# The last attention stage of a two-layer block: block 0's queries placed by TensorE, and the router and wide products of the end spread over the last slots

## What is computed

```python
x = x + _L0_xattn_ref(_layernorm(x), ...)
x = x + _L0_ffn_ref(_layernorm(x), ...)
x = x + _L1_xattn_ref(_layernorm(x), ctx_2048, Wq, Wk, Wv)
x = x + _L1_ffn_ref(_layernorm(x), W, bias, rw1, rb1, rw2, rb2, A, B, gates)
# _L1_xattn_ref: 32 heads of 8 channels
q = _rmsnorm(q); k = _rmsnorm(k)
attn = softmax(einsum('bhnd,bhmd->bhnm', q, k) * 8 ** -0.5)
out = einsum('bhnm,bhmd->bhnd', attn, v)
# _L1_ffn_ref: the router, and the low-rank correction
h = silu(x @ rw1.T + rb1)
logits = (h @ rw2.T + rb2)[:, :16] + gates
topv, topi = top_k(logits, 2); sm = softmax(topv)
coeff = zeros_like(logits).at[rows, topi].set(sm)
base = x @ W.T + bias
xa = einsum('ni,eri->ner', x, A)
out = base + einsum('ner,eor->no', xa * coeff[:, :, None], B)
```

## Time and profile before

| | us |
|---|---|
| median of 3 runs (380.56 to 381.72) | 381.45 |
| the profiled execution's own time | 378.31 |
| its span, first to last instruction | 376.2 |
| busy in it: PE, DVE, ACT, POOL | 291.7, 274.7, 174.6, 100.8 |
| stage C, from its first query product to the last slot's last output product | about 251 to 337 |
| the end, to the span's end | about 337 to 376 |

### The profile page before, as it was taken

How to read it: one execution, slowest core, us unless ns; L and a number is a source line. 1 busy time by engine, 2 the same in 40 slices (tenths; PEclk the granted TensorE clock), 3 DMA queues, 4 the chain that set the end, 5 groups by cost and what they waited for, 6 DMA issues and landing times.

```text
span 376.2 us, 7252 instructions
## 1 busy us (share of the span) xinstructions
PE 291.7 (78%) x2636; PEld 182.2 (48%) x2636; DVE 274.7 (73%) x706; ACT 174.6 (46%) x296; POOL 100.8 (27%) x200
## 2 busy tenths in 40 slices
PE   4246888878887876899996998954888884978795
PEld 3112444344443333586775887831555552553543
DVE  6977789889898886778922643455588887686894
ACT  1102365665756666535333677413576665430101
POOL 1134254463543222202770211077101000000000
PEclk9855599999999999969996999985799999877999
DMA  7583359568585103100236477765756555100011
GB/s 248 159 260 113 92 159 281 155 194 274 151 255 154 46 24 134 46 2 21 92 112 195 133 254 263 262 186 161 218 161 198 172 157 164 49 3 0 0 56 56
DMA packets 70306, 53.20 MB, mean 141 GB/s; under 512 B 4864, under 2 KB 67072, under 8 KB 70272
## 3 DMA queue, kind: packets, MB, share of 16 engines
q1 hardware_dynamic: 64640, 41.76, 36.8%
q10 hardware_dynamic: 4096, 6.79, 5.7%
q0 software_dynamic: 1536, 4.20, 3.5%
HBM read 30.90 MB, written 21.63 MB: 140 GB/s over the span
## 4 chain that ended last, share of the span: by engine, by line
PE 38%; DVE 34%; DMA 8%; issue 8%; POOL 5%; ACT 4%; SPq 2%; DVEq 0%; POOLq 0%
DVE mx L1589 8%; PE psum L689 5%; PE psum L1027 4%; POOL sorted_x L1496 4%; PE psum L725 4%; PE psum L1040 4%; PE psum L674 3%; PE psum L710 2%; DVE pvT L1941 2%; DMA qstk<-mT 2%; ACT prob L1177 2%; PE psum L1003 2%; PE psum L816 2%; DVE rope_ab L1578 2%; PE psum L1136 2%
## 5 line engine op out<-in xcount | busy, mean ns | idle before, releaser
L1589 DVE TENSOR_REDUCE mx<-psum 128x2 f32<-128x512 f32 x128 | 81.3, 684 | 16.1 <-PE psum L689 15.3
L1177 ACT ACTIVATE prob<-psum 128x1024 f32<-128x1024 f32 x64 | 64.4, 1023 | 39.7 <-PE psum L710 39.4
L689 PE MATMUL psum<-kstk,qstk 64*128 64x256 bf16 x256 | 27.9, 300 | 26.7 <-DVE mx L1589 14.5
L725 PE MATMUL psum<-prob,vt 128*32 128x256 f32 x512 | 35.2, 392 | 6.2 <-ACT prob L1177 5.1
L1361 ACT ACTIVATE prob<-psum 128x1024 f32<-128x1024 f32 x32 | 31.9, 1019 | 13.2 <-PE psum L987 13.2
L689 PEld LDWEIGHTS psum<-kstk,qstk 64*128 64x128 bf16 x256 | 8.8, 98 | 43.6 <-DVE mx L1589 28.1
L484 POOL TENSOR_TENSOR parts<-qk_rest,parts 128x256 bf16<-128x256 f32 (+1 forms) x15 | 13.7, 913 | 51.0 <-ACT parts L1335 47.2
L710 PE MATMUL psum<-qstk,kstk 64*128 64x256 bf16 x256 | 25.1, 281 | 1.2 <-DMA qstk<-mT 1.2
L1003 PE MATMUL psum<-prob,vt 128*32 128x128 f32 x512 | 21.7, 292 | 4.6 <-ACT prob L1361 4.6
L725 PEld LDWEIGHTS psum<-prob,vt 128*32 128x32 f32 x512 | 14.2, 110 | 18.7 <-ACT prob L1177 7.6
L1027 PE MATMUL psum<-low,qstk 128*128 x124 | 18.6, 297 | 2.0 <-issue 1.9
(11 more groups left out here) (256 smaller groups left out, 610.2 us busy)
## 6 DMA issues: line engine op xcount, KB each, us to landing
qstk<-stack_scratch SPq DMA_DIRECT2D x32, 256.0 KB, 3.7
stack_scratch<-parts SPq DMA_DIRECT2D x23, 192.0 KB, 2.2
kstk<-key_scratch SPq DMA_DIRECT2D x16, 256.0 KB, 3.9
kstk<-stack_scratch SPq DMA_DIRECT2D x14, 256.0 KB, 5.7
stack_scratch<-parts SPq DMA_DIRECT2D x25, 128.0 KB, 2.1
low<-in_wup ACTq DMA_DIRECT2D x4, 640.0 KB, 4.6
wdn<-in_wdn ACTq DMA_DIRECT2D x4, 640.0 KB, 5.8
prob<-sorted_x SPq DMA_DIRECT2D x8, 256.0 KB, 4.3
```

The source lines that it names most:

```text
L689: last = nc.tensor.matmul(banks[s][:, nb * D:(nb + 1) * D], qstk[par][rows, pair, nb * P:(nb + 1) * P], kstk[par][rows, pair, :], start=Tr ...
L725: last = nc.tensor.matmul(pv_bank(1)[32 * j:32 * j + 32, g * D:(g + 1) * D], vt[b % 2][:, mb, 4 * t + j, 8:40] if low else vt[b % 2][:, mb ...
L1177: nc.scalar.activation(prob[(b * PAIRS + k) % 3][:], exp_buf(k).rearrange("p a n -> p (a n)"), ACT.Exp, scale=SCALE).then_inc(exp_done, 1)
L1589: nc.vector.tensor_reduce(mx[:, half, :, 4 * s + p4:4 * s + p4 + 1], bank.rearrange("n (b m) -> n b m", b=2), AX_X, ALU.max).then_inc(misc ...
```

## The change

Start of stage C:

- Block 0's queries no longer pass through DRAM. A table `place` of zeros and ones (GpSimd makes it early, beside `work_no`) is multiplied with each of the three parts by TensorE, 24 matmuls of 32 rows x 128 x 256 (`place_queries`), so that the stack's rows arise in PSUM, banks 4 to 7. ScalarE copies groups 0 and 2 and VectorE groups 1 and 3 into `qstk` (`stack_placed`). SyncE's loop over queries begins at block 1.
- The steps of `C_PRO` have PSUM banks of their own and another order: q of block 1 ahead of qT of block 0; qT of block 1 and xT of block 2 behind the placing; the first score product ahead of q of block 2. On VectorE the sums of squares stand ahead of `add_shared(2)`, and the statistics and centring of block 2 behind both copies of the stack.

Slots 5 to 7 and the end:

- The reciprocal root of the dense layer's norm starts from logarithm, exponential and square on ScalarE (`guess_ln`), with two steps on VectorE behind it (`ln_roots`) in place of ten. Statistics of blocks 0 to 3 are taken at slot 5's first spot, those of 4 to 6 in slot 7, block 7 alone behind the slots.
- Transposed blocks are copied by ScalarE (`take_dxT`) and not by VectorE. Wide products of blocks 0, 1 and 2 are made in slots 6 and 7, and ScalarE copies them out to SBUF (`take_wide`). The router's hidden layer is made for blocks 0 to 3, for 4 and 5, and for 6 and 7.
- GpSimd adds the bias and, for blocks 0 to 2, the base to `xall` (`based`). The two rows that were added to the logits one after the other are added to each other early.
- The order behind the slots is another on TensorE, ScalarE and VectorE.

```diff
-        C_PRO = [("v", 0), ("xT", 0), ("q", 0), ("xT", 1), ("qT", 0), ("q", 1), ("xT", 2), ("qT", 1), ("q", 2)]
+        C_PRO = [("v", 0), ("xT", 0), ("q", 0), ("xT", 1), ("q", 1), ("qT", 0), ("qT", 1), ("xT", 2), ("q", 2)]
+        C_GONE = [("v", 0), ("xT", 0), ("xT", 1), ("q", 0), ("qT", 0), ("q", 1), ("qT", 1), ("xT", 2), ("q", 2)]
+        C_BANK = {("v", 0): 4, ("xT", 0): 5, ("q", 0): 6, ("xT", 1): 0, ("q", 1): 1, ("qT", 0): 2, ("xT", 2): 3,
+                  ("qT", 1): 2, ("q", 2): 4 + (B_END + 8) % 2}
...
-        D_EARLY = {(5, 6): ("dxT", 0), (5, 7): ("dxT", 1), (6, 1): ("dxT", 2), (6, 2): ("dxT", 3),
-                   (6, 6): ("dh", 0), (7, 3): ("dlg", 0)}
+        D_EARLY = {(5, 5): ("dxT", 0), (5, 7): ("dxT", 1), (6, 1): ("dxT", 2), (6, 3): ("wide", 0), (6, 5): ("dxT", 3),
+                   (6, 7): ("dh", 0), (7, 1): ("wide", 1), (7, 3): ("dlg", 0), (7, 5): ("wide", 2)}
...
-            for b in range(NB):
+            for b in range(1, NB):
...
+            def place_queries(part, made):
+
+                pe.wait_ge(made, NB + 1)
+                for g, kp in itertools.product(range(4), range(2)):
+                    rows = slice(32 * g, 32 * g + 32)
+                    last = nc.tensor.matmul(psum[:, 4 + g, kp * D:(kp + 1) * D],
+                                            place[rows, part, 16 * kp:16 * kp + 16, :].rearrange("c l t -> c (l t)"),
+                                            parts[0][rows, 0, part, :], start=(part == 0 and kp == 0), stop=(part == 2),
+                                            skip_group_check=True)
+                    if part == 2 and kp == 1:
+                        last.then_inc(placed, 1)
...
+            pro_use("v", 0)
+            pro_use("xT", 0)
+            pro_use("q", 0)
+            pe.wait_ge(relu_done, 3 * N_SHARED)
+            pro_use("xT", 1)
+            pro_use("q", 1)
...
+            pro_use("qT", 0)
...
+            place_queries(0, hi_done)
+            place_queries(1, mid_done)
+            place_queries(2, lo_done)
+            pe.wait_ge(misc_free, pro_gone("q", 1))
+            pro_use("qT", 1)
+            pro_use("xT", 2)
...
             scores_c(0, 0)
+            pro_use("q", 2)
...
+            ring("dxT", 4)
+            ring("dxT", 5)
+            ring("dxT", 6)
+            ring("o")
...
-            pe.wait_ge(misc_free, C_END)
-            wide(0)
-            wide(1)
-            ring(("o",))
+            wide(3)
+            ring("dh", 1)
+            wide(4)
+            ring("dxT", 7)
+            ring("dh", 2)
+            wide(5)
+            ring("dlg", 1)
             pe.wait_ge(pv_free, 3 * NB + 2)
-            wide(2)
-            wide(3)
-            ring(("dxT", 4))
             flip_wxa(0)
-            ring(("dxT", 5))
             flip_wxa(1)
             delta(0)
-            ring(("dxT", 6))
+            delta(1)
+            wide(6)
             flip_wxa(2)
-            delta(1)
-            ring(("dxT", 7))
-            ring(("dh", 1))
             flip_wxa(3)
             delta(2)
+            ring("wide", 7)
             delta(3)
-            wide(4)
-            wide(5)
-            ring(("dlg", 1))
-            wide(6)
-            wide(7)
             flip_wxa(4)
...
+            squares(0, pro_full("q", 0), pro_bank("q", 0))
+            guess_roots(0)
+            squares(1, pro_full("q", 1), pro_bank("q", 1))
+            pro_split(0)
+            guess_roots(1)
+            for g in (0, 2):
+                stack_placed(g)
+            pro_split(1)
+            squares(2, pro_full("q", 2), pro_bank("q", 2))
+            guess_roots(2)
...
+            def take_wide(b):
+                key = slot_of("wide", b)
+                act.wait_ge(misc_full, late_full(key))
+                nc.scalar.copy(raw(b), late_bank(key)).then_inc(x_copied, 1)
...
+                nc.scalar.activation(ln_log[:, blocks], ln_v[:, blocks], ACT.Ln).then_inc(ln_step, 1)
+                act.wait_ge(ln_step, 3 * j + 1)
+                nc.scalar.activation(ln_g[:, 0, blocks], ln_log[:, blocks], ACT.Exp, bias=lead[:], scale=-0.5
+                                     ).then_inc(ln_step, 1)
+                act.wait_ge(ln_step, 3 * j + 2)
+                nc.scalar.activation(ln_g[:, 1, blocks], ln_g[:, 0, blocks], ACT.Square).then_inc(ln_step, 1)
...
+                    if shape == 5 and k == 3:
+                        guess_ln(0, 0, 4)
+                        take_dxT(0)
+                    if shape == 6 and k == 0:
+                        take_dxT(1)
+                    if shape == 6 and k == 1:
+                        take_dxT(2)
+                    if shape == 6 and k == 2:
+                        take_wide(0)
+                    if shape == 6 and k == 3:
+                        take_dxT(3)
...
+                        silu_exp(0)
+                    if shape == 7 and k == 1:
+                        take_wide(1)
                     if shape == 7 and k == 3:
+                        take_wide(2)
                         gap_exp(0)
...
+            guess_ln(1, 4, 3)
+            for b in range(4, 7):
+                take_dxT(b)
+            silu_exp(1)
+            guess_ln(2, 7, 1)
+            take_dxT(7)
+            silu_exp(2)
+            take_wxa(0)
+            take_wxa(1)
             gap_exp(1)
...
+                rows_g = slice(32 * g, 32 * g + 32)
+                steps.then(nc.gpsimd.tensor_copy(place[rows_g, part, :, first:first + n],
+                                                 eye16[rows_g, rows_g].unsqueeze(2).broadcast_to((32, 32, n))))
...
+                last = nc.gpsimd.tensor_tensor(xall[:, b, :], xall[:, b, :], rows[:, 4 * NE:4 * NE + D], ALU.add)
+                if b < N_RAW:
+                    steps.then(last)
+                    pool.wait_ge(x_copied, gone_a(slot_of("wide", b)))
+                    last = nc.gpsimd.tensor_tensor(xall[:, b, :], xall[:, b, :], raw(b)[:, 0:D], ALU.add)
+                last.then_inc(based, 1)
...
             center(1, 1)
+            sum_squares(0)
+            c_pro(("xT", 1))
+            scale_queries(0, pro_bank("q", 0))
             add_shared(2)
-            c_pro(("q", 0))
-            c_pro(("xT", 1))
+            sum_squares(1)
             c_pro(("qT", 0))
-            attend_norm(2, 1)
+            scale_queries(1, pro_bank("q", 1))
+            add_experts(2, 1)
+            c_pro(("qT", 1))
+            for g in (1, 3):
+                stack_placed(g)
+            attend_norm(2, 1, added=True)
             center(2, 0)
-            c_pro(("q", 1))
             c_pro(("xT", 2))
-            c_pro(("qT", 1))
             c_pro(("q", 2))
...
+                nc.vector.tensor_scalar(ln_v[:, blocks], mv[:, blocks, 1], float(HD), HD * LN_EPS, ALU.mult, ALU.add
+                                        ).then_inc(ln_ready, 1)
...
+                dve.wait_ge(ln_step, 3 * j + 3)
+                steps.then(nc.vector.tensor_tensor(rs_a[:, blocks], ln_v[:, blocks], ln_g[:, 1, blocks], ALU.mult))
+                steps.then(nc.vector.scalar_tensor_tensor(out=rstd[:, blocks], in0=rs_a[:, blocks], scalar=3 * HD / KAPPA,
+                                                          in1=ln_g[:, 0, blocks], op0=ALU.subtract, op1=ALU.mult,
+                                                          reverse0=True))
...
+                    if shape == 5 and spot == 0:
+                        ln_stats(0, 4)
+                    if shape == 5 and spot == 4:
+                        ln_roots(0, 0, 4)
+                        ln_normalize(0)
+                        ln_normalize(1)
+                    if shape == 6 and spot == 0:
+                        ln_normalize(2)
+                    if shape == 6 and spot == 2:
+                        ln_normalize(3)
+                    if shape == 7 and spot == 1:
+                        silu(0)
+                    if shape == 7 and spot == 4:
+                        dve.wait_ge(misc_free, gone_v((7, "o")))
+                        ln_stats(4, 3)
                         weights_of(0)
+                        ln_roots(1, 4, 3)
+                        for next_ in range(4, 7):
+                            ln_normalize(next_)
...
+            c_use("o", 1, late_wait((NB, "o")), NB - 1)
+            dve.wait_ge(misc_free, gone_v((NB, "o")))
+            ln_stats(7, 1)
             weigh(1)
-            ring(("dxT", 4))
-            ring(("dxT", 5))
             weigh(2)
-            ring(("dxT", 6))
+            ln_roots(2, 7, 1)
+            ln_normalize(7)
+            silu(1)
+            silu(2)
             weigh(3)
-            ring(("dxT", 7))
-            for b in range(4):
-                add_bias(b)
+            picks(1)
...
-            ring(("dh", 1))
+            weights_of(1)
+            weigh(4)
             finish(2)
-            finish(3)
-            for b in range(4, NB):
-                add_bias(b)
-            ring(("dlg", 1))
-            for b in range(4, NB):
```

(6 more changed lines are left out.)

352 lines of the change are left out of this document (215 added, 137 removed).

## The result

| | executions | us, median | range |
|---|---|---|---|
| before | 4 | 381.0 | 380.56 to 381.72 |
| after | 4 | 375.82 | 374.49 to 377.83 |

The ratio is 0.9898 (95% interval 0.9851 to 0.9945). Two more comparisons gave 0.9873 (0.9827 to 0.9919) and 0.9924 (0.9891 to 0.9957). Over 63 executions of before from the later comparisons and 22 of after the medians are 380.2 and 376.2 (executions more than 1.5% above the fastest of their kernel are left out of these and of all ratios). So the change is worth some 4 us. I had put down 0.6, and 375.82 lies outside my range of 378.0 to 383.2.

The account below looks back on a forecast made before the run. Bound by a chain of small waiting steps at stage C's start, and by VectorE, then TensorE's transposes and low-rank products, at the end. Start +1.9 and end -2.5 gave -0.6: 381.45 to 380.85 us, range 378.0 to 383.2.

Parts of the forecast that it names:

- The start: Start of stage C: third q at 267.3 instead of 265.23, a loss taken as 1.9 us that passes through whole.
- Eight of 32 rows for a part are then 0.86: Placing block 0's queries: eight 32-row matmuls per part take 0.86, pairs overlapping; third part placed from 260.2 to 261.2.
- Rival 2: Start: 32-row placing does not overlap, third part ends at 263.4, start loses 3.9; total 382.85 us; chance 0.17.
- block 2's centring ... what was early is now last: VectorE at the start: block 2's centring, behind the stack's copies, ends at 265.8 where it ended at 260.45.
- Slots 5 to 7: First dxT 1.6 earlier through fewer root steps; wide products and ScalarE copies make the silu of blocks 0 to 3 1.8 later.
- The adds on GpSimd ... cost nothing: Slots and end: GpSimd's adds lie up to ten us ahead of their use and cost nothing.
- Behind the slots: Router's last product at 357.45 to 358, not 362.54: 5.1 gained; TensorE's work before the second half gives 2.6 back.
- The end as a whole: Slots 5 to 7 and the stretch behind them together: -2.5 us (-3.8 to -1.9 depending on TensorE's clock).
- Its own time is 3.1 below the median ... I take the sum as a difference: Profiled execution of before took 378.31; the -0.6 sum was applied to the median of 381.45 instead.
- Rival 1: q, placing and wide 3 run at 2.4 GHz: start +0.6, end -3.8, total 378.25 us; chance 0.33.
- Rival 3: ScalarE's order delays block 7's second part and stack read before slot 7; end loses 2.6, total 383.45 us; chance 0.06.
- Rival 4: Walk behind the slots too dear, weighing and low-rank products interleave better: end -4.5, total 378.85 us; chance 0.04.

Follow-up runs that it names:

- start_only: Kernel before with only the new start of stage C (new order of first uses, block 0's queries placed by TensorE); 380.46 us, ratio 1.0002.
- roots_alone_t2: Second trace of the kernel before with only the last norm's roots moved to ScalarE; this execution 378.61 us, the kernel's median 377.52, ratio 0.9901.
- end_only: Changed kernel with the old start order and block 0's queries through DRAM, each q waiting only for its own transposed rows; 374.35 us, ratio 0.9842.
- centre_exp: Changed kernel, block 2 normed and centred ahead of the stack's copies, first exponential ahead of block 2's squares and roots; 373.20 us, ratio 0.9848.
- no_wide: Changed kernel with the wide products of slots 6 and 7, and block 7's, cut to 16 of 512 columns; 375.19 us, ratio 0.9886.
- best: Changed kernel with both orders of centre_exp, plus the router's first product of blocks 4 and 5 ahead of block 3's wide product; 372.78 us, ratio 0.9778.

## Why the prediction was wrong, step by step

**The start, "+1.9 (0.6 to 3.9)": right in sign, too large by about 0.9.** By the medians of eight and seven traces it is +1.0; start_only has +1.0, the repeats of after +1.1 to +1.5, and the first trace +2.5, where the clock stayed low. (The walk itself came to 2.1; that I took 1.9 has no term behind it.)
- "qT of block 0 ... 257.0": it starts 6.26 behind C0 (254.68 - 248.42), not 6.76, since the second q started 4.39 behind C0 and not 4.76. That is even 0.1 earlier than in before; the 0.4 that I charged wasn't there.
- "Eight of 32 rows for a part are then 0.86": eight take 0.63 at 0.50; less the tail of a group (0.17 by the text) that is 0.46, or 0.058 each. My bound without overlap was 0.215 each, 3.7 times as much, so nearly four ran at once. The third part was placed 9.8 behind C0 (256.79 + 1.39 - 248.42), not 11.0. That is what the Trainium skill (TensorEngine Tiling, Theoretical Speedup and Key Properties) says of 32-row tiles; by its sentence I had put the loss at 1.5 and set it aside for the row on pairs. Rival 2 (no overlap) is excluded.
- "The transfer ... is already hidden": so in six of the seven traces with the old start, but not in roots_alone_t2 (1.17), nor in end_only, where q came earlier (1.84).
- "block 2's centring ... what was early is now last": right, and shown by centre_exp. The third q came 1.1 later, not 2.1: the placing was done 1.2 earlier than in the walk, and the centring gave 0.5 of that back, as it took 0.87 beside a GpSimd add and not 0.35. "Passes through whole": right, from q on.

**Slots 5 to 7, "1.6 gained" and "1.8 lost".** The first late transpose gained 2.0 (7.22 behind S5 before, 5.22 in after). The silu came 1.1 to 2.0 later behind S5 where the clock fell (18.3 to 19.2; 17.27 in the trace of before, 17.3 to 18.5 in its five), and 0.4 earlier in the one execution where it didn't. The walk stands for the usual case. Z-D: 14.3 predicted (the terms as listed add up to 14.15), 14.76 measured. The difference is a term that I had put at nothing: "The adds on GpSimd ... cost nothing". In all ten traces with the new end one norm ahead of the last division took 0.82 beside GpSimd's adds and 0.41 without them, and a step of the last division took 0.47, against 0.29 in earlier divisions of after (325.23, 329.69). Together that is 0.6.

**Behind the slots, "5.1 gained" and "2.6 given back": right, against the trace that they were worked out from.** D-R was 11.3 to 11.85 by the text and is 11.3 to 12.3 in the traces. From R to the first transposes of the second half I had 8.65 and the trace 8.66 (365.14 - 356.48); tail 5.4 and 5.47. "TensorE, not VectorE, busy until the flip of block 4": so it is, and no_wide confirms it.

**The end as a whole, "-2.5": the step that failed.** The new end itself came out near the forecast: the text's walk gives 58.8 for S5-E (374.06 - 2.5 - 312.76), and the six traces with that end unchanged have 57.1, 58.8, 58.9, 60.1, 60.2 and 60.5, 59.2 on average; against the usual 60.2 of after it was 1.4 too short. But I held it against one execution of before, 61.3, and that was the kindest of the six with the old end (63.2 on average). I let TensorE's clock fall in the new end behind the last division, and took the old end as it stood in that trace, with no fall in its tail. By the averages the end is worth **-4.0**; by the kindest of each (61.3 and 57.1) and by their usual ones (64.4 and 60.2) it is -4.2. (The five traces of before and the four of after alone give -3.4.) With +1.1 for the start, by the means of the same eight and seven traces, that makes -2.9. A further 0.2 to 0.3 stood in no term of mine: an execution's own time is 2.0 to 2.2 longer than its span in the five of before, and 1.7 to 1.9 in the four of after (2.0 and 1.8 by the medians of 63 and 22). I had carried the 2.1 over. That makes -3.1 to -3.2 of the 4.0; the 0.8 to 0.9 that is left is smaller than the narrowest interval (1.3 either way), and its cause stays open.

**"Its own time is 3.1 below the median ... I take the sum as a difference": the same mistake, seen from outside.** The 3.1 was not a constant of the measurement. 2.8 to 3.4 of S5-E lie between that trace and the two at the median (64.13 and 64.67 less 61.30): 1.3 in the tail, 0.6 in S5-S6, 0.6 to 0.8 in D-R, 0.4 to 0.6 in S6-Z. Part of it was hidden from the total, since the first trace reached C0 1.1 and 2.1 later than those two (250.24; 249.19 and 248.16). The change takes away the wait behind which the tail's clock fell. Of 63 executions of before the median had 79.0 us at 1.2 GHz (twice the span times one minus the mean clock), the profiled one 75.2, and of 22 of after the median 74.9.

**The rivals.** Rival 1 (the clock is kind, 378.25, 0.33) had the direction, but not what it put it down to: q and the placing ran at 0.50 (2.08 for q), and so did most of wide 3 (0.50 up to 348 in after). The clock mattered in the old end, where it didn't look. Rival 3: nothing waited for a `qstk` transfer in slot 7. Rival 4 (the walk too dear behind the slots): no. None of them had the old kernel's usual execution as its term.

## What to carry to other kernels

A trace of before is one draw. Where the gap between its own time and the median is several times the change that you forecast, ask which stretches could make it up (look for TensorE waits that happened to be followed by a clock of 1.00, here 2.49 and 2.86 long), price the old kernel in its usual state too, and compare like with like. A wait that a change removes may be worth more than its length if the clock can fall behind it (here 1.3 more for the wait of 2.49, in five of eight traces). A small operation that is moved to GpSimd isn't free while VectorE works on its chain beside it. A transfer that is hidden today can be the next thing waited for. And when a transfer leaves a chain, look at what now stands last on each engine: a changed order on VectorE and ScalarE took 1.7 to 2.7 off the start in the two traces that have it (centre_exp, best).

## What the runs showed of the hardware that I had not expected

- The same wait of TensorE in the same program is followed by either clock from one execution to the next: 2.86 by 1.00 or 0.50 in slot 5 (2.3 us), 2.49 by 1.00 or 0.50 in the old tail (1.3 us).
- Nearly four matmuls of 32 rows and 256 columns ran at once, 0.058 us each at 1.2 GHz.
- VectorE's centring of 128x256 took 0.87 (262.36) where a GpSimd add of 0.69 ran beside it (262.38), 0.86 to 0.87 in the seven other traces of this order, and 0.35 in centre_exp and best, where none ran beside it. A norm of the same size took 0.82 beside GpSimd's adds and 0.41 without (342.42 and 350.87). The Trainium skill (SBUF — State Buffer, SBUF: two separate sides) has VectorE and GpSimd share a port pair that one holds for a whole instruction; these traces agree with it.
- A lead of 5.5 us of ScalarE's first exponential was worth no more than the 1.7 of the third q, with TensorE at 1.2 GHz in between; that the clock is the reason isn't shown.
- The same read-back from DRAM was waited for in one of seven executions with the same order (1.17 us), and the stack of block 1 in another (0.67 us).
